# Attention B's 64 steps written out instead of looped, and two VectorE pieces of attention A in another order

## What is computed

```python
x = x + attn_a(layernorm(x))   # 32 heads of 16, 8 kv groups, no mask, 1024 x 1024 scores a head
x = x + ffn(layernorm(x))      # base matmul plus a rank-16 mixture of 2 of 8 experts
x = x + attn_b(layernorm(x))   # 4-bit weights with scales, 32 heads of 128, 8 kv groups, rotary, causal
x = x + ffn(layernorm(x))
```

## Time and profile before

| | us |
|---|---|
| median of 3 runs | 1618.2 |
| lowest and highest | 1615.97, 1626.73 |
| the profiled execution's own time | 1621.11 |
| its span in the trace | 1619.3 |

### The profile page before, as it was taken

The page is one execution under the profiler, slowest core; times in us unless marked ns, Lnnn a source line. Parts: engine busy times, 40 slices in busy tenths (PEclk is TensorE's granted clock), DMA queues, the critical chain, the costliest instruction groups (busy, mean ns, idle before and its releaser), DMA issues.

```text
span 1619.3 us, 25526 instructions
## 1 busy us (share of the span) xinstructions
PE 1480.0 (91%) x7932; PEld 700.4 (43%) x7932; DVE 1239.5 (77%) x2583; ACT 868.7 (54%) x1468; POOL 237.6 (15%) x174
## 2 busy tenths in 40 slices
PE   5789999999998998899998988998988999999979
PEld 3412323233332354455554544554544544555534
DVE  4288888888886378787897877897877886877863
ACT  2205767666766423565565554674654664655631
POOL 2102000000000042211212211212212221211020
PEclk8958999999999999899999999999999999999999
DMA  3993000000000323467576566675675674653631
GB/s 94 153 141 120 1 1 0 0 0 0 0 0 0 72 79 104 98 131 144 124 136 132 125 119 129 135 142 117 127 134 115 130 156 98 136 103 63 104 66 52
DMA packets 352266, 144.96 MB, mean 90 GB/s; under 512 B 314680, under 2 KB 324408, under 8 KB 352128
## 3 DMA queue, kind: packets, MB, share of 16 engines
q1 hardware_dynamic: 352144, 143.48, 42.9%
HBM read 59.64 MB, written 6.19 MB: 41 GB/s over the span
## 4 chain that ended last, share of the span: by engine, by line
PE 71%; DVE 12%; issue 6%; ACT 4%; DMA 4%; SPq 2%; ACTq 0%; DVEq 0%; POOL 0%
PE ps L1444 9%; PE ps L1446 9%; PE ps L1445 9%; PE ps L1226 9%; PE ps L1279 7%; PE ps L1265 6%; PE ps L1406 3%; PE ps L1525 3%; PE ps L1527 3%; PE ps L1526 3%; DMA hlT<-hl 2%; DVE mx L834 2%; SPq L470 2%; PE ps L1369 2%; DMA scratch<-pieces 2%
## 5 line engine op out<-in xcount | busy, mean ns | idle before, releaser
L834 DVE TENSOR_REDUCE mx<-ps 128x1 f32<-128x512 f32 x512 | 327.7, 686 | 66.6 <-PE ps L1226 64.4
L683 ACT ACTIVATE x<-ps,nmb,factor 128x128 f32<-128x128 f32 (+7 forms) x256 | 211.7, 832 | 304.3 <-DVE nmb L1034 304.3
L592 ACT ACTIVATE proj<-ps 128x1024 f32<-128x1024 f32 x256 | 248.5, 1021 | 121.6 <-PE ps L1265 120.7
L1226 PE MATMUL ps<-ks,qs 96*128 (+1 forms) x512 | 199.7, 413 | 30.9 <-DVE pieces L859 15.1
L1049 DVE SCALAR_TENSOR_TENSOR hl<-x,rden,hl 128x128 f16<-128x128 f32 (+7 forms) x256 | 208.1, 813 | 14.7 <-issue 10.8
L691 ACT ACTIVATE hl<-x,rden 128x128 f16<-128x128 f32 (+7 forms) x256 | 184.1, 767 | 27.0 <-DVE rden L1045 26.3
L1032 DVE TENSOR_REDUCE nmr<-ps 128x1 f32<-128x128 f32 (+7 forms) x256 | 191.5, 748 | 0.0
L511 POOL TENSOR_TENSOR tmp<-tmp 128x640 f32<-128x640 f32 x64 | 98.5, 1539 | 554.7 <-DVE tmp L1028 554.7
L1444 PE MATMUL ps<-wh,xTh 128*128 128x256 f16 (+1 forms) x512 | 168.5, 329 | 1.7 <-issue 1.7
L1445 PE MATMUL ps<-wl,xTh 128*128 128x256 f16 (+1 forms) x512 | 168.3, 329 | 0.0
L1446 PE MATMUL ps<-wh,xTl 128*128 128x256 f16 (+1 forms) x512 | 168.2, 329 | 0.0
(11 more groups left out here) (155 smaller groups left out, 2150.5 us busy)
## 6 DMA issues: line engine op xcount, KB each, us to landing
scale<-sp_n SPq DMA_DIRECT2D x32, 384.0 KB, 4.2
st<-in_L_attn_b_qw_q_dram SPq DMA_DIRECT2D x32, 256.0 KB, 2.6
st<-in_L_attn_b_qw_o_dram SPq DMA_DIRECT2D x32, 256.0 KB, 2.8
scale<-so_n SPq DMA_DIRECT2D x32, 256.0 KB, 3.4
qs<-scratch SPq DMA_DIRECT2D x24, 256.0 KB, 8.3
hlT<-hl SPq DMA_TRANSPOSE x256, 3.4
scratch<-pieces SPq DMA_DIRECT2D x5, 768.0 KB, 13.0
xnat<-attn_a_hidden_state_dram SPq DMA_DIRECT2D x8, 256.0 KB, 5.2
```

The source lines that it names most:

```text
L592: nc.scalar.activation(pbuf[:, e % 4, :].rearrange("p (b n) -> p b n", b=2), ps[:, b:b + 2, :], ACT.Exp, scale=float(HD) ** -0.5).then_inc ...
L683: nc.scalar.activation(pr[:, h, 0:n], flat(2 * (h % 2), n), ACT.Exp, bias=nmb[:, h:h + 1], scale=factor[:, par, 0:1], accum_out=den[:, h:h ...
L834: nc.vector.tensor_reduce(mx[:, f, k // 2, k % 2:k % 2 + 1], ps[:, bank(k), :], AX.X, ALU.max).then_inc(s_mx, 1)
L1226: mm(ps[:, bank, :], qs[0:STACK, ds(g * R + h, 1), f * HALF + qt * P:f * HALF + (qt + 1) * P], ks[0:STACK, ds(g, 1), kh * HALF:(kh + 1) * ...
```

## The change

Attention B: `steps` runs all 64 steps as written-out code on every engine, with constant counts, and SyncE waits without `hold`. Attention A: VectorE's `normalise` stands behind maxima 0 to 3 instead of 0 to 5, and in the last group `normalise_scales` behind `normalise` instead of ahead of it.

```diff
-        def steps(step, eng):
-
-            for t in range(T - 1):
-                step(0, t, 0)
-            with eng.Fori(0, G // 2 - 1) as gg:
-                for g, t in [(0, T - 1)] + [(1, t) for t in range(T)] + [(2, t) for t in range(T - 1)]:
-                    step(gg * 2 + g, t, g % 2)
-            for g, t in [(G - 2, T - 1)] + [(G - 1, t) for t in range(T)]:
-                step(g, t, g % 2)
+        def steps(step):
+
+            for g in range(G):
+                for t in range(T):
+                    step(g, t, g % 2)
...
-            def hold(what, count):
-
-                if not isinstance(count, int):
-                    count = sp.to_reg(count)
-                sp.wait_ge(s_tab, 48)
-                sp.wait_ge(what, count)
-
...
-                    hold(s_dq, g2 * CHUNKS + c - 1)
-                    hold(s_wlp, g2 * CHUNKS + c - STAGES + 1)
+                    sp.wait_ge(s_dq, g2 * CHUNKS + c - 1)
+                    sp.wait_ge(s_wlp, g2 * CHUNKS + c - STAGES + 1)
...
-                    hold(s_lo, u * R + h + 1)
+                    sp.wait_ge(s_lo, u * R + h + 1)
...
                     if not last:
-                        maxima(u + 2, f, 0, 6, in_ring)
-                    elif f == 0:
-                        normalise_scales()
-                    else:
+                        maxima(u + 2, f, 0, 4, in_ring)
+                    elif f == 1:
                         weight(KC - 1)
...
                     if not last:
-                        maxima(u + 2, f, 6, MM, in_ring)
+                        maxima(u + 2, f, 4, MM, in_ring)
                     else:
+                        if f == 0:
+                            normalise_scales()
                         for n in (range(KC - 1), range(KC, KC + 3))[f]:
                             weight(n)
```

More of the change, by code:

```diff
@@ L462, in step @@
                 if not (isinstance(g2, int) and g2 >= G):
-                    hold(s_dq, g2 * CHUNKS + c - 1)
-                    hold(s_wlp, g2 * CHUNKS + c - STAGES + 1)
+                    sp.wait_ge(s_dq, g2 * CHUNKS + c - 1)
+                    sp.wait_ge(s_wlp, g2 * CHUNKS + c - STAGES + 1)
                     load_chunk(g2, c)
                 for h in range(R):
-                    hold(s_lo, u * R + h + 1)
+                    sp.wait_ge(s_lo, u * R + h + 1)
                     if h == 0 and exists(*before(g, t, 2)):
-                        hold(s_pvb, u - 1)
+                        sp.wait_ge(s_pvb, u - 1)
                     sp.dma_start_transpose(hlT[t % 2][:, h, 0:2 * (t + 1), :],
                                            hl[:, h, 0:2 * (t + 1) * P]).then_inc(s_tp[h], 16)
-            steps(step, sp)
+            steps(step)
             for t in range(T):
@@ L531, in _ @@
             rope_add(0)
-            steps(step, pool)
+            steps(step)
             add_base_bias(xnat, 3, bb)
@@ L714, in _ @@
             tokens(2, 6, 7)
-            steps(step, act)
+            steps(step)
             root(3, 0)
@@ L1138, in _ @@
             low_tokens(6, 7)
-            steps(step, dve)
+            steps(step)
             final_statistics(2, 3)
@@ L1555, in _ @@
             tokens(2, 6, 7)
-            steps(step, pe)
+            steps(step)
             output_first(G - 1, T - 2, (G - 1) % 2)
```

## The result

The changed kernel takes 1568.4 us (median of 4 runs, 1567.15 to 1571.05); the kernel before, run beside it, 1621.0 (4 runs, 1615.97 to 1626.73). The ratio is 0.970, with a 95% interval of 0.967 to 0.973. The forecast was 1579, the range 1568 to 1596: the time came out at the range's fast end, 0.4 us inside it. The profiled execution took 1571.05, with a span of 1569.2 against 1619.3.

What follows compares the result with a forecast made beforehand. TensorE was taken to bound both attentions, so only its idle time pays: 15.1 + 8.8 + 15.4 = 39.3 us off the profiled 1621.1 gives 1581.8; that execution lay 2.9 above the median, hence 1579, range 1568 to 1596.

Steps and rivals of the forecast that it cites:

- The division behind the fourth maximum: Attention A, 13 units: TensorE's whole wait for VectorE's division goes and no new one follows, 15.1 us.
- B's scales behind the division: A's last group: TensorE's wait of 7.14 us goes, and 1.7 us of slow clock with it, 8.8 us in sum.
- The branches: Attention B's loop: two taken branches go, each making a step 6 longer by 5.08 us, 10.2 us in all.
- The third rival: B's branches: other waits are served at that place and come up without it, nothing saved, 1589 us; chance 0.05.
- The registers in steps 1 to 3: B, six groups: register arithmetic before waits goes, 0.15 us in each of 18 steps, 2.7 us.
- Step 0: B's group boundaries: TensorE's wait for SyncE's transposes shortens without register work, 0.5 us in five groups, 2.5 us.
- The clock: B's group boundaries: TensorE's granted clock, low at four of six looped boundaries, 6.7 us in all, was kept as it was.
- If it stayed up everywhere, 1572: B's group boundaries: full clock at all of them, 6.7 us; the clock rival, either way, had chance 0.14.
- The likeliest case: Whole kernel: all terms come as forecast with the clock as before, 1573 to 1586 us; chance 0.63.
- The fourth rival: B written out: straight code must be fetched and stalls, 5.1 us a time, up to 82 us, 1661; chance 0.04.

Runs made afterwards that it cites:

- norm5: The changed kernel with A's division behind the fifth maximum instead of the fourth: 1577.1 us, ratio 0.979 to the kernel before.
- a_only: Both edits of attention A, with B's steps looped as in the kernel before: 1587.7 us, ratio 0.984 to the kernel before.
- sp_loop: The changed kernel with SyncE alone looped again in B, with `hold`: 1573.0 us, ratio 0.976 to the kernel before.
- a_out: The changed kernel with attention A's hardware loops written out too, on every engine: 1574.3 us, ratio 0.975 to the kernel before.
- b_only: B's steps written out, with attention A in its old order as in the kernel before: 1595.9 us, ratio 0.988 to the kernel before.
- dve_loop: The changed kernel with VectorE alone looped again in B: 1576.6 us, ratio 0.977 to the kernel before.
- fill: The changed kernel plus six matmuls with discarded results in TensorE's step 0 of groups 1 to 7: 1568.9 us, ratio 0.972 to the kernel before.
- a_out_fill: The changed kernel with A's loops written out and six discarded matmuls in step 0 of groups 1 to 7: 1568.8 us, ratio 0.972 to the kernel before.
- shift: The changed kernel with four extra VectorE copies of 128x512 ahead of B, to move B in time: 1568.8 us, ratio 0.972 to the kernel before.
- act_loop: The changed kernel with ScalarE alone looped again in B: 1572.6 us, ratio 0.976 to the kernel before.
- pe_loop: The changed kernel with TensorE alone looped again in B: 1578.7 us, ratio 0.980 to the kernel before.
- dve_pe_loop: The changed kernel with VectorE and TensorE looped again in B, the others written out: 1585.8 us, ratio 0.982 to the kernel before.

## Why the prediction was right, and where it was short

**The division behind the fourth maximum: right in kind, mis-sized by 1.7 us.** All 13 waits went and none came up at the next maxima; norm5 shows that one reduction more brings half of it back. The term "Gain: the 13 waits, 15.1 us" should be 16.8. It took the wait from 318.56, an end which the profile models; the next matmul could have started 0.14 earlier, as the trace after shows. 13 x 0.14 = 1.8, and 1.7 came.

**B's scales behind the division: right.** Forecast 8.8, measured 8.3 for the last group's two units. The wait went whole, and no slow stretch follows it.

**The branches: right.** Forecast 10.2, measured 9.9. The 5.08 us a branch was read from step 6 alone; step 7 behind it gives 0.2 back when the branch goes (16.99 to 17.22). The runs with one engine looped say whose they are: VectorE's 3.45, TensorE's 1.0 to 1.5, ScalarE's and SyncE's nothing when alone; GpSimd's was not tried. The third rival (nothing saved) fell. The Trainium skill's rule on taken branches ("Runtime: NRT & Kernel Launch", Instruction fetch mechanics), by which the engine waits for a fetch when the target is outside the fetched window, was rightly preferred. The traces agree by the size of the stall, 4.3 us on VectorE alone; that it is a fetch they don't show.

**The registers in steps 1 to 3: right.** Forecast 2.7; measured 2.3 in steps 1 to 3 and 0.4 in steps 4 and 5, where I had counted nothing. In steps 1 to 3 it is made up of ScalarE's 0.08 and TensorE's 0.06 a step. I had not said which engine's; VectorE's, on the chain of these steps too, cost nothing.

**Step 0: mis-sized, and for a wrong reason.** Forecast 2.5, from "I take 0.5 in five groups". The looped step 0 at full clock is 0.75 to 0.8 longer in a_only, so the term is 3.8 or 3.9, as much as the idle time of the seven steps fell. "SyncE's register work stands between the last softmax row and its DMA" was the reason given; sp_loop gives that 0.1 a step.

**The clock: the step that failed.** "I keep it as it was." The rival "If it stayed up everywhere, 1572" is what came, and at its full size: TensorE's busy time in B fell by 9.6 us with the same matmuls. Without them B gave 9.9 + 2.7 + 3.8 = 16.4 against the forecast's 15.4, and the whole change would have given about what was forecast. The 6.7 us of that rival were counted on four boundaries from single rows of steps 0; the accounting above has some 8 in steps 0 and 1.7 in step 2 of group 6, which I had not looked at. For the profiled execution the sum gave 1581.8 and 1571.05 came, 10.8 less: A gave 1.2 more than forecast, B 11.0 more, 9.6 of it clock, and what lies outside the marks of A and B took 1.4 us longer than before.

The forecast had this rival, at a chance of 0.14, and nothing in the prediction's working made it the likely case. The likeliest case alone had 1573 to 1586, and the time isn't in it. That it lies inside the whole range, by 0.4 us, is luck as far as the main case goes.

Why the clock stayed up is open. The idle time at the boundary may have a part in the fall: with a_out's filled, the low clocks of steps 0 were gone. But among kernels with nearly the same idle times one falls and another doesn't. Of the seven boundaries the profiled executions show at a low clock: none in the changed kernel, b_only, norm5, dve_loop, fill, a_out_fill and shift, one in a_only and sp_loop, three in act_loop and pe_loop, four in the kernel before and dve_pe_loop, and all seven in a_out. So B written out on all engines had none in six kernels of seven, and the seventh had all. What decides was not found. The change's own part in the 9.6 us is not shown, only that they came with it.

A part of the 52.6 us between the two medians is the kernel before's own clock. A run of it takes 1608 to 1627, and the forecast and the result rest on its slowest batch: there its median was 1621.0, later 1611.9 to 1614.6. The two kernels whose B is nearest to the changed one's, fill and shift, stood 46 us below it in the third batch (1568.9 and 1568.8 against 1614.6), not 53.

**The fourth rival** (straight code must be fetched and stalls) fell. No step of B is longer than before by more than 0.3 us, and the chain's issue share went from 6% to 3%.

## What to carry to other kernels

Where several engines share one ring of buffers, put each consumer into its engine's order at its place in the ring; each reduction of 0.62 us ahead of it cost its full time in every unit. The hardware loop with B's long body cost VectorE a stall of 4.3 to 5.8 us at each taken branch and TensorE 3.7 to 4.2, and little of TensorE's showed (1.0 to 1.5); A's loop, with a quarter of the matmuls in its body, shows no such piece in the chain. Look for "issue" at the branch's line, and price it by the step with the branch against the same step without one. When the bound is TensorE, keep a term for its clock in the sum, since 10 us of it came and went here beside idle times of a microsecond, as much as the branches were worth. And read a profiled execution as one draw: that of the kernel before took 1621.1 us, 6 to 9 above the kernel's medians in the later batches.

## What the runs showed that I had not expected

- The profile's end of a matmul of two tiles lies 0.14 us behind the point at which the next can start (0.45 between starts against 0.59), so an idle time behind it is undercounted by that.
- A taken branch's stall on VectorE depends on who branches with it: 4.31 us alone, 5.22 with TensorE, 5.52 (a_only) and 5.73 with all engines.
- Waits on a register's value cost TensorE 0.06 and ScalarE 0.08 us a step of B, VectorE nothing. In A the loops of all engines together cost 0.39 us a unit of the loop.
- Six matmuls that do nothing useful, at full clock 1.3 us of TensorE's time, left a step of 14.1 us as long as it was.
- The mean clock of the same program differs from one execution to the next: a_out took 1563.6 at a mean clock of 0.976 and 1574.9 at 0.965.
